# Two transformer layers for sixteen sequences in one slot schedule: norms on ScalarE, experts every third slot, the shared expert's products in the next batch's slots, two residual buffers

## The reference

```python
xn = layernorm(x)
x = x + attention0(xn) + ffn0(xn)     # softmax attention, 16 heads of 8; fp4-rounded gated FFN, 352 wide
xn = layernorm(x)
x = x + attention1(xn) + moe(xn)      # linear attention (elu+1 features), 16 heads; experts, 344 wide
```

## Time and profile before

| | us |
|---|---|
| median of three runs (2304.74 to 2309.8) | 2307.14 |
| the profiled execution's own time | 2310.34 |
| its span, first to last instruction | 2308.5 |
| PE busy, share of span | 2078.7, 90% |
| DVE busy | 1635.0, 71% |
| ACT busy | 1400.3, 61% |
| POOL busy | 1147.4, 50% |
| mean granted PE clock | 0.971 |

### The profile page before, as it was taken

How to read it: one execution, slowest core, us unless ns; L and a number is a source line. 1 busy time by engine, 2 the same in 40 slices (tenths; PEclk the granted TensorE clock), 3 DMA queues, 4 the chain that set the end, 5 groups by cost and what they waited for, 6 DMA issues and landing times.

```text
span 2308.5 us, 52509 instructions
## 1 busy us (share of the span) xinstructions
PE 2078.7 (90%) x18761; PEld 1355.0 (59%) x18761; DVE 1635.0 (71%) x5384; ACT 1400.3 (61%) x3797; POOL 1147.4 (50%) x1800
## 2 busy tenths in 40 slices
PE   3888989989899998989989899998989999898988
PEld 1455655656566574655656566574655656566565
DVE  7557767677777767767677776767767677766756
ACT  1667566665756657566665756657566575756642
POOL 5675463745536454463645636454463745535220
PEclk7779999999999999999999999999999999999999
DMA  4000000000000000000000000000000000000000
GB/s 119 6 6 2 1 15 1 15 2 11 6 2 15 1 15 2 1 15 2 15 2 7 10 2 15 2 15 2 1 15 2 15 2 11 1 2 11 2 10 6
DMA packets 33542, 22.03 MB, mean 10 GB/s; under 512 B 2443, under 2 KB 32771, under 8 KB 33283
## 3 DMA queue, kind: packets, MB, share of 16 engines
q1 hardware_dynamic: 33283, 18.68, 2.8%
HBM read 14.48 MB, written 4.19 MB: 8 GB/s over the span
## 4 chain that ended last, share of the span: by engine, by line
PE 60%; DVE 16%; ACT 13%; issue 8%; POOL 4%; DVEq 0%; ACTq 0%; POOLq 0%
PE ps L1097 9%; PE ps L1168 9%; PE ps L1178 7%; PE ps L1237 7%; PE ps L1111 6%; ACT ring L921 4%; PE ps L1087 3%; PE ps L1066 3%; DVE ring L538 3%; ACT pb L930 3%; PE ps L1075 2%; PE ps L1222 2%; PE ps L1144 2%; PE ps L1195 2%; PE ps L1207 2%
## 5 line engine op out<-in xcount | busy, mean ns | idle before, releaser
L814 POOL TENSOR_SCALAR ring<-ring,row_rcp,tau_row 128x128 f32<-128x128 f32 (+3 forms) x1024 | 626.1, 618 | 824.4 <-DVE row_rcp L545 824.2
L921 ACT ACTIVATE ring<-ring,neg_max 128x128 f32<-128x128 f32 (+3 forms) x1024 | 572.2, 560 | 625.6 <-DVE neg_max L538 622.3
L1097 PE MATMUL ps<-identf,ring 128*128 128x128 f32 x2560 | 384.9, 288 | 17.9 <-ACT qkT L912 11.3
L930 ACT ACTIVATE pb<-ps 128x512 f32<-128x512 f32 x640 | 349.1, 585 | 23.9 <-PE ps L1097 16.8
L538 DVE CUSTOM_DVE_ANT_1 ring<-ps,bias_t 128x384 f32<-128x384 f32 (+1 forms) x496 | 287.2, 615 | 82.3 <-PE ps L1087 78.3
L1097 PEld LDWEIGHTS ps<-identf,ring 128*128 128x128 f32 x2560 | 280.1, 144 | 103.8 <-issue 62.6
L1168 PE MATMUL ps<-xn1T,eg_t 128*128 128x512 f32 (+1 forms) x480 | 265.1, 635 | 37.2 <-DVE h L592 36.9
L1237 PEld LDWEIGHTS ps<-ed_t,h 128*128 128x128 f32 (+1 forms) x1920 | 250.7, 191 | 74.7 <-issue 73.1
L1237 PE MATMUL ps<-ed_t,h 128*128 128x128 f32 (+1 forms) x1920 | 272.3, 278 | 0.0
L1178 PE MATMUL ps<-xn1T,eu_t 128*128 128x512 f32 (+1 forms) x480 | 259.3, 622 | 0.4 <-DVE h L599 0.4
L944 ACT ACTIVATE tanh_t<-ps 128x512 f32<-128x512 f32 (+2 forms) x304 | 171.9, 565 | 123.0 <-PE ps L1168 118.3
(11 more groups left out here) (161 smaller groups left out, 3208.2 us busy)
## 6 DMA issues: line engine op xcount, KB each, us to landing
x_t<-x SPq DMA_DIRECT2D x16, 256.0 KB, 2.8
x<-x SPq DMA_DIRECT2D x16, 256.0 KB, 2.8
out<-x SPq DMA_DIRECT2D x16, 256.0 KB, 2.3
bias_t<-bias SPq DMA_DIRECT2D x1, 1536.0 KB, 7.7
eg_t<-eg SPq DMA_DIRECT2D x1, 860.0 KB
eu_t<-eu SPq DMA_DIRECT2D x1, 860.0 KB
ed_t<-ed SPq DMA_DIRECT2D x2, 320.0 KB
ring<-inv_row SPq DMA_DIRECT2D x1, 256.0 KB, 2.7
```

The lines of the kernel that those rows point to most:

```text
L814: pool.tensor_scalar(e, e, row_rcp[:, m % 2, r:r + 1], tau_row[:, i, HG * g + r:HG * g + r + 1], ALU.mult, ALU.add).then_inc(p_ok.sem, 1)
L921: act.activation(e, e, ACT.Exp, bias=neg_max[:, n % 2, r:r + 1], scale=-1.0, accum_out=row_sum[:, n % 2, r:r + 1]).then_inc(exp_ok.sem, 1)
L930: act.activation(pb[:, c % NPB, :], bank(turn_bank(q)), ACT.Relu).then_inc(t_taken[q % 2].sem, 1)
L1097: last = pe.transpose(o[:, r * P:(r + 1) * P], ring_of(i, r)[:, k * P:(k + 1) * P], idf)
```

## The change

- `norm` moves from DVE to ACT: DVE now writes only `shift = -mean * rstd` (one 128x4 instruction, `norm_shift`), and ACT four `Identity` activations with scale and bias, at the same places (2, and `ADD_X1 + 3`).
- `ADD_X1` goes from `L1 + 14` to `L1 + 13`, and with it the statistics, `rstd` and second norm.
- `GATE1` goes from every 2.5 slots from `L1 + 25` to every third from `L1 + 26`; the last unit is at `L1 + 68`, which is slot 4 of the next frame. `DOWN1` is written out per tile; the shared expert's four products are at `L1 + 78, 81, 84, 88`: slots 14, 17, 20 and 24 of the next frame. The Y bank's order is now counted by the plan.
- `pv` of first tiles (`i == 0`) comes four slots behind its `turn_probs`, not two.
- `elu_m` has three buffers, and `elu_high`, `stack_high` and `stack_low` of layer 1 come one slot later.
- DVE's and POOL's fp4 steps of `x` come one slot later, `HID_AMAX` goes to 18, 19, 34, 35, `STACK0` from 27 and 59 to 26 and 58, `FUTURE_V` and `FUTURE_Y` from slots 61 and 63 to slots 1 and 3 of the next frame.
- `x1` has two buffers with a semaphore each, loaded a frame earlier. The last frame has 26 slots instead of 8.

```diff
-STACK0 = (27, 45, 59, 69)
-HID_AMAX, HID_STEP, HID_SCALED = [p + 3 for p in GATE0], 36, (38, 39, 40, 41)
+STACK0 = (26, 45, 58, 69)
+HID_AMAX, HID_STEP, HID_SCALED = (18, 19, 34, 35), 36, (38, 39, 40, 41)
-TURN_H, FUTURE_V, FUTURE_Y = (ATT + 11, ATT + 13, ATT + 13, ATT + 15), ATT + 61, ATT + 63
-WO, WO_LAST, ADD_X1 = (L1 + 7, L1 + 8, L1 + 9, L1 + 11), L1 + 12, L1 + 14
+TURN_H, FUTURE_V, FUTURE_Y = (ATT + 11, ATT + 13, ATT + 13, ATT + 15), ATT + 65, ATT + 67
+WO, WO_LAST, ADD_X1 = (L1 + 7, L1 + 8, L1 + 9, L1 + 11), L1 + 12, L1 + 13
-GATE1 = [L1 + 25 + 5 * u // 2 for u in range(3 * NE)]
-DOWN1 = [GATE1[3 * e + 2] + 4 for e in range(NE - 1)] + [L1 + 65]
+GATE1 = [L1 + 26 + 3 * u for u in range(3 * NE)]
+DOWN1 = [tuple(L1 + p for p in places) for places in ((36, 37, 39, 40), (48, 49, 50, 51), (55, 57, 59, 60), (63, 65, 65, 66), (78, 81, 84, 88))]
+TAIL = DOWN1[E][T - 1] + 2 - 2 * SLOTS - SLOTS
...
-        return self.blocks(*divmod(SLOTS * f + s - 2, SLOTS))
+        near, far = (self.blocks(*divmod(SLOTS * f + s - back, SLOTS)) for back in (2, 4))
+        return [blk for blk in far if STEPS[blk[1]][1] == 0] + [blk for blk in near if STEPS[blk[1]][1]]
...
-        x1 = sb("x1", [P, T, D])
+        x1 = sb("x1", [P, 2, T, D])
+        shift = sb("shift", [P, 2, T])
-        elu_m = sb("elu_m", [P, 2, 2 * D])
+        elu_m = sb("elu_m", [P, 3, 2 * D])
...
-            def norm(b, layer, src, dst):
+            def norm_shift(b, layer):
                 dve.wait_ge(rstd_ok[layer].sem, rstd_ok[layer].at(b, 1))
-                for t in range(T):
-                    dve.tensor_scalar(dst[:, t, :], src[:, t, :], moments[:, layer, t, 0:1], rstd[:, layer, t:t + 1],
-                                      ALU.subtract, ALU.mult).then_inc(xn_ok[layer].sem, 1)
+                dve.scalar_tensor_tensor(out=shift[:, layer, :], in0=moments[:, layer, :, 0], scalar=-1.0, in1=rstd[:, layer, :],
+                                         op0=ALU.mult, op1=ALU.mult).then_inc(shift_ok[layer].sem, 1)
...
-                if 0 <= p - QKV1 - 4 < T:
-                    elu_high(b, p - QKV1 - 4)
+                if 0 <= p - QKV1 - 5 < T:
+                    elu_high(b, p - QKV1 - 5)
...
-                    if p == DOWN1[e] + 4:
+                    if p == DOWN1[e][T - 1] + 1:
                         accumulate(b, e)
...
+            def norm(b, layer, src, dst):
+                act.wait_ge(shift_ok[layer].sem, shift_ok[layer].at(b, 1))
+                for t in range(T):
+                    act.activation(dst[:, t, :], src[:, t, :], ACT.Identity, bias=shift[:, layer, t:t + 1],
+                                   scale=rstd[:, layer, t:t + 1]).then_inc(xn_ok[layer].sem, 1)
...
+                if p == 2:
+                    norm(b, 0, x_t, xn)
+                if p == ADD_X1 + 3:
+                    if has(b + 2):
+                        act.wait_ge(t_ps.sem, plan.turn["xq", b + 2, 0] + 1)
+                    norm(b, 1, x1[:, b % 2, :, :], xn1)
...
-                    pe.wait_ge(y_taken.sem, y_taken.at(b, e + 1))
+                    pe.wait_ge(y_taken.sem, plan.y[e, b])
...
                 for e in range(NE):
-                    if 0 <= p - DOWN1[e] < T:
-                        down1(b, e, p - DOWN1[e])
+                    for t in range(T):
+                        if p == DOWN1[e][t]:
+                            down1(b, e, t)
```

More of the change, by code:

```diff
@@ L100, in __init__ @@
         self.nb = nb
-        self.turn, self.score, self.g_ps, self.g_taken = {}, {}, {}, {}
+        self.turn, self.score, self.g_ps, self.g_taken, self.y = {}, {}, {}, {}, {}
         self.units, taken = [], [0, 0]
@@ L131, in __init__ @@
                         gate_ticket(("up", layer, b, places.index(p - 1)), 1)
+                if p == WO_LAST:
+                    self.y["first", b] = len(self.y)
+                for e in range(NE):
+                    if p == DOWN1[e][T - 1]:
+                        self.y[e, b] = len(self.y)
         self.unit = {key: n for n, key in enumerate(self.units)}
@@ L138, in slots @@
         for f in range(-1, self.nb + 2):
-            for s in range(SLOTS if f <= self.nb else 8):
+            for s in range(SLOTS if f <= self.nb else TAIL):
                 yield f, s
@@ L289, in build @@
         rstd_ok = two("rstd_ready")
+        shift_ok = two("norm_shift_ready")
         xn_ok = two("xn_ready", T)
@@ L701, in urgent @@
                 if p == 2:
-                    norm(b, 0, x_t, xn)
+                    norm_shift(b, 0)
                 if 0 <= p - QKV0 - 1 < T:
@@ L705, in urgent @@
                 if p == ADD_X1:
[L706 to L708 removed]
+                    dve.wait_ge(y_ps.sem, plan.y["first", b] + 1)
+                    dve.wait_ge(x1_in[b % 2].sem, x1_in[b % 2].at(b // 2, 16))
+                    dve.tensor_tensor(x1[:, b % 2, :, :], x1[:, b % 2, :, :], bank(Y).rearrange("p (t d) -> p t d", t=T),
                                       ALU.add).then_inc(y_taken.sem, 1)
                 if p == ADD_X1 + 1:
[L711 to L712 removed]
+                    dve.wait_ge(y_taken.sem, plan.y["first", b] + 1)
+                    norm_stats(b, 1, x1[:, b % 2, :, :])
                 if p == ADD_X1 + 3:
[L714 to L716 removed]
+                    norm_shift(b, 1)
                 if 0 <= p - QKV1 - 1 < T:
                     rope(b, 1, p - QKV1 - 1)
[L719 to L720 removed]
+                if 0 <= p - QKV1 - 5 < T:
+                    elu_high(b, p - QKV1 - 5)
                 if 0 <= p - QKV1 - 2 < T:
@@ L1189, in down0 @@
             def down0(b, t):
-                if t == 0 and b:
-                    pe.wait_ge(y_taken.sem, y_taken.at(b, 0))
+                if t == 0 and plan.y["first", b]:
+                    pe.wait_ge(y_taken.sem, plan.y["first", b])
                 wait_turned(("hid", b, t))
```

69 lines of the change are left out of this document (31 added, 38 removed).

## The result

| | before | after |
|---|---|---|
| median, us | 2305.94 (2302.63 to 2309.8) | 2278.95 (2277.89 to 2279.86) |
| the profiled execution's own time | 2310.34 | 2279.62 |
| its span | 2308.5 | 2277.8 |

The ratio is 0.9882, with a 95% interval of 0.9865 to 0.9899: 27 us, or 1.2%, faster. The forecast was 2232. The kernel is faster, as forecast, and the time lies in the range of 8 in 10 (2196 to 2288), but outside the forecast's own 2205 to 2260; of the forecast change of the profiled execution (75 us) only 31 came. It is close to where rival A ended (2274).

The account below looks back on a forecast made before the run. PE's own work (about 127 us a frame) plus its waits was the bound. 6.5 us removed less 2.0 returned gave 4.5 a frame, 68 over 15 frames; with 8 for the clock and 1 lost, a 2232 us median, range 2196 to 2288.

Parts of the forecast that it names:

- rival A: Removed waits move to PE's next waits; two thirds come back, 2.2 us a frame remain, 2274 us; chance 0.18.
- the sum: Over a steady frame: 6.5 us of PE waits removed, 2.0 returned, so 4.5 us gained.
- Kept: PE waits taken to stay as they are, per frame: `lin` 1.54 us, stack copies 0.75, `vx` 0.72.
- Start of the frame, no change counted: Slots 0 to 5: PE gains about 3 us of work, DVE about 9.5 busy stays under PE's 12.9; priced at nothing.
- The clock's 8 us: With idle time of slots 14 to 26 filled, some slow-clock stretches vanish: 8 us in total (0 to 16).
- Experts every third slot: Gates' two waits a frame for `silu` go, because PE has at least one more slot of work between: 2.4 us.
- `pv` two slots later: First tiles' wait for `store_o`, at most 0.8 us long, is covered by two slots: 0.75 us a frame gone.
- Slots 14 to 19: Waits for `silu`, `hidden` and the second norm go, 3.35 us a frame; 1.5 return (ADD 0.8, norm 0.4, `hidden` 0.3).
- The 0.3 for `hidden`: Slots 14 to 19: 0.3 us a frame booked for what is left of PE's waits for `hidden`.
- Norms on ACT: Four activations take 1.6 us at 0.39 each (bounds 0.3 to 0.8), hidden in slot 2; no table load added.
- The elu chain: `stack_low` of layer 1 one slot later, PE's first turn still in slot 31: 0.5 us a frame returned (0 to 1.5).
- Ends: Kernel end: only the last unit's own up product covers its tanh, `silu` and `hidden`, 1 us more; start the same.

Follow-up runs that it names:

- a4: Changed kernel with expert gates (every 2.5 slots) and down products back at their old places, all else changed: 2260.05 us.
- b3: Kernel before with only the new `GATE1`, `DOWN1` and `ADD_X1` places and their buffers: 2281.56 us.
- b1: Kernel before with only `pv` of first tiles later, four slots behind instead of two: 2303.76 us.
- a2: Changed kernel with `pv` of first tiles two slots behind again: 2270.19 us.
- c2: Changed kernel with five down products moved to cover waits for `lin`, the stack copy and the product at slot 14: 2240.67 us.
- e1: Changed kernel with only `fv` and `fy` back at slots 61 and 63 of the frame before: 2263.15 us.
- e2: Changed kernel with only `fv` and `fy` moved to slots 25 and 27, from 1 and 3 of the next frame: 2233.82 us.
- a3: Changed kernel with layer 1's elu chain one slot earlier, as before the change, keeping three elu buffers: 2279.1 us.
- d3: c4 with `FUTURE_V` and `FUTURE_Y` moved to slots 25 and 27: 2194.81 us.
- c3: c2 with the first two gates two slots later and the next two one slot later: 2253.71 us.
- d1: c4 with half the heads left out of ACT's casts for layer 1's stack, a timing-only run with wrong results: 2226.44 us.
- d2: c4 with k's half left out of DVE's layer 1 rope products, a timing-only run with wrong results: 2219.32 us.
- c1: Changed kernel with the shared expert's `accumulate` on DVE moved eight slots later, from slot 25 to 33: 2278.65 us.
- c4: c2 with the norm of layer 1 back on DVE, that of layer 0 staying on ACT: 2230.15 us.

## Why the prediction was wrong in size

The step that failed is the sum, and in it the price of what comes back: 2.0 us a frame returned were booked, and 4.2 returned. Two terms of it were put at nothing and were not: "Kept", and "Start of the frame, no change counted". The other step that failed is taking each removed wait at its full length, also in slots 20 to 31. The clock's 8 us did not come either. By the prediction's own steps, in us per clean frame:

- **Experts every third slot, 2.4 gone: the waits yes, the time no.** No gate waits for an expert's `silu`. But 1.3 of the 2.4 lay in slots 20 to 31, whose length did not move, and a4 shows that gates and products together, as the change places them, cost 0.7 a frame beside the rest. Alone they gave 1.1 (b3's clean frame is 136.31).
- **`pv` two slots later, 0.75 gone:** true of the wait. By clean frames it is worth 0.56 in the kernel before (b1) and 0.28 in the changed one (a2); neither run's time shows it.
- **Slots 14 to 19, 3.35 removed, 1.5 returned: right.** All of it went and 0.69 + 0.46 = 1.15 came back. The ADD (L717) ends at 1129.71, the product starts at 1129.81, which is why I read its wait as the one for bank Y, though the profile names no releaser (0.8 forecast, 0.69 measured; c2 has the product one slot later and no such wait):

```profile
1128.59 0.52 DVE L601 SCALAR_TENSOR_TENSOR hid<-tanh_t,ps 128x352 f32<-128x352 f32 x1 [3.13 <-ACT tanh_t L951]
1129.03 0.68 DVE L717 TENSOR_TENSOR x<-x,ps 128x512 f32<-128x512 f32 x1
...
1129.81 0.46 PE L1254 MATMUL ps<-wout_t,qT 128*128 128x128 f32 x2 [0.69 <-issue]
```

  The 0.3 for `hidden` did not come.
- **Norms on ACT, 1.6 for four: right.** Four take 1.64 us. There is still one table load, of 1283 ns. By the Trainium skill (ScalarE: Activation LUTs, "Table sets: the hidden batching unit") identity belongs to every set, and the trace agrees. All Identity instructions and the load, in ns min/median/max:

```profile
L960 ACT ACTIVATE xn<-x_t,shift,rstd x64: 478/480/493, 9.4 to 1924.7; 128x128 f32<-128x128 f32 x64
L960 ACT ACTIVATE xq<-x,shift,rstd x64: 478/485/493, 181.7 to 2203.8; 128x128 f32<-128x128 f32 x64
L960 ACT ACT_TABLE_LOAD  x1: 1283/1283/1283, 8.1 to 8.1; - x1
```

- **Start of the frame, no change counted: wrong.** `fv` and `fy` in slots 1 and 3 cost 1.05 a frame against their old place (e1) and 2.2 against slots 25 and 27 (e2). I added up busy times of PE and DVE; both fitted. But `fy` takes a score bank, DVE empties it (`y_future`) behind other work, and the next scores wait 0.43; the waits cut groups of products in two, and with that PE's busy time grew by 0.8 as well.
- **The elu chain, 0.5: 0.28** in the trace; a3's time is the same, but its dips differ.
- **Kept, 1.54 + 0.75 + 0.72 unchanged: wrong for two of three.** `lin` went from 18.5 to 22.1 us in twelve frames, the turn for the stack copy on ACT from 9.0 to 12.4, with 4.6 and 4.3 for DVE's copy and `nd` beside it. Only `vx` stayed at 8.7.
- **Sum: 6.5 removed, 2.0 returned.** PE's waits in the list fell from 10.8 to 8.5 a frame, so against 6.5 removed 4.2 came, net: the returned term is the one that failed. Booked and measured are 0.69 + 0.46 + 0.28. Unbooked are `kv` 1.40, the turns at slot 48 0.64, 0.43 + 0.38 + 0.28 at slots 0 to 6, `lin` 0.3, slot 62 0.17; three waits of 0.3 at slot 4 (0.84) went unbooked too, which leaves 4.2. That a wait would "move" was rival A, given 0.18; its 2.2 us a frame is near what the frame shows (1.96).
- **Clock, 8 us: nothing came.** 10 dips became 8 in twelve frames. From 286.1 to 2086.0, 13 frames of the kernel before, the excess over 137.41 is 13.6 us; in the changed kernel (277.6 to 2052.5, over 135.45) 14.1. The forecast expected dips to go with the idle time of slots 14 to 26. But the dip that it read at 1170.9 begins at the end of the 1.32 us wait of a gate in slot 27 (L1168). That wait went, and so did the dips behind it, but others came behind the wait for `lin` at slot 44 (last section).
- **Ends:** the last frame costs 2.8 us, not 1, though it has 3.4 us at clock 0.50 where the one before has 13.7; at the same clock it would cost more. The wait at the last unit's first product is 1.34 where the earlier trace rows has 0.77; in the first two frames the change gains 8.2 where two of the forecast's frames would give 9.

The span sums: -0.4 before the first scores, -8.2 in two frames, -25.0 in thirteen, +2.8 behind: -30.7, the difference of the spans. At 4.5 and a clock term of 8 the thirteen would have been -66.

What stays open: which chain sets the 22.3 us of slots 20 to 31. It isn't the sum of any engine's work there: 1.1 us more of PE's (d3, e2) and 1.8 less (c3) moved the length by 0 and -0.35, 1.6 less of ACT's (d1) by -0.16 and 1.8 less of DVE's (d2) by -0.26. But c1, with only 0.67 us of DVE's work taken out at slot 25, moved it by -0.59, so DVE's queue from there on is part of the chain; what stands before it isn't shown. The wait for `vx` at slot 22 is 0.72 before and after and in c4, e1 and e2, which fits an order q/k/v, `vx` and rope, elu, stack; no run shortened that order itself, so this is argued, not shown.

## What to carry to other kernels

Ask of each stretch whether its bound is the engine that you relieve, before you add up its waits. Where two other engines were as busy as PE (19.3, 19.2 and 19.0 of 22.3 us here), taking 2.07 us of waits away gave nothing, but the same slots took 1.1 us more of its work for free: move work in (e2, two numbers, 2%), and cover waits in the stretches that the engine does bound (c2). And a product moved to a place "with room" on PE also takes a bank there, which another engine must empty.
